# Two reordered places and POOL's divisions in a two-layer attention and expert kernel

## What is computed

```
block 0: linear attention, 32 heads of 64
block 1: mixture of experts
block 2: softmax attention, 32 query heads of 8, 8 key/value heads
    scores = einsum(q, k) / sqrt(8);  attn = softmax(scores)
    out = einsum(attn, v);            return out @ Wo + bo
block 3: mixture of experts
    expert = argmax(x @ router);  xs = x * sigmoid(max logit)
    out = (silu(xs @ gate[e]) * (xs @ up[e])) @ down[e]      for each token's expert e
    shared = (silu(x @ sgate) * (x @ sup)) @ sdown;          return out + shared
```

## Time and profile before

| | us |
|---|---|
| median of 3 runs | 669.4 |
| lowest, highest of them | 667.64, 670.4 |
| profiled execution, device time | 665.62 |
| its span (first to last instruction) | 663.9 |
| PE, DVE, ACT, POOL busy in the span | 615.3, 400.0, 328.4, 208.7 |
| TensorE's granted clock, mean of the span | 0.983 |

### The profile page before, as it was taken

The page is one execution under the profiler, slowest core; times in us unless marked ns, Lnnn a source line. Parts: engine busy times, 40 slices in busy tenths (PEclk is TensorE's granted clock), DMA queues, the critical chain, the costliest instruction groups (busy, mean ns, idle before and its releaser), DMA issues.

```text
span 663.9 us, 11796 instructions
## 1 busy us (share of the span) xinstructions
PE 615.3 (93%) x4298; PEld 407.6 (61%) x4298; DVE 400.0 (60%) x929; ACT 328.4 (49%) x654; POOL 208.7 (31%) x304
## 2 busy tenths in 40 slices
PE   3999999999999988999879999999999999999980
PEld 2887887888888785566566444444444445556650
DVE  5426705632760577443377989888899955743335
ACT  4523423433332234254315588898988875423321
POOL 5870661282074064313422122111010100431331
PEclk9999999999999999999979999999999999999995
DMA  6100200300199996314199996000000000031213
GB/s 221 33 1 33 96 1 25 102 1 1 34 272 271 119 176 223 105 48 120 69 296 335 270 155 4 1 2 1 2 1 2 1 2 1 17 106 47 84 53 126
DMA packets 69000, 57.40 MB, mean 86 GB/s; under 512 B 21520, under 2 KB 64400, under 8 KB 68944
## 3 DMA queue, kind: packets, MB, share of 16 engines
q1 hardware_dynamic: 66736, 50.60, 34.0%
q0 software_dynamic: 2208, 6.05, 2.5%
HBM read 30.78 MB, written 25.85 MB: 85 GB/s over the span
## 4 chain that ended last, share of the span: by engine, by line
PE 76%; DVE 15%; ACT 3%; DMA 2%; issue 2%; POOL 2%; ACTq 0%; POOLq 0%; SPq 0%; DVEq 0%
PE psum L303 9%; PE psum L305 9%; PE psum L304 9%; PE psum L1296 8%; PE psum L1641 8%; DVE mx L1751 7%; PE psum L1325 5%; PE psum L1613 5%; PE psum L1601 5%; PE psum L1626 3%; PE psum L1289 3%; DVE stat L652 2%; PE psum L1220 2%; PE psum L1571 2%; PE psum L1305 1%
## 5 line engine op out<-in xcount | busy, mean ns | idle before, releaser
L1751 DVE TENSOR_REDUCE mx<-psum 128x1 f32<-128x512 f32 x256 | 157.7, 683 | 17.5 <-PE psum L1613 17.4
L1512 ACT ACTIVATE pr<-psum 128x512 f32<-128x512 f32 x256 | 137.8, 599 | 28.2 <-PE psum L1626 26.4
L1641 PE MATMUL psum<-pr,vals 128*32 128x256 f32 x1024 | 77.6, 389 | 0.0
L1626 PE MATMUL psum<-qT,kT 32*128 32x512 f32 x256 | 76.5, 494 | 0.7 <-ACT pr L1512 0.7
L1613 PE MATMUL psum<-kT,qT 32*128 32x512 f32 x256 | 67.7, 489 | 1.7 <-ACT qT L1479 0.7
L1296 PE MATMUL psum<-w_gu,xgT 128*128 x120 | 56.4, 592 | 0.0
L610 POOL DMA_INDIRECT routed_y<-yr,xg x30 | 28.8, 958 | 87.8 <-DVE yr L862 87.2
L1613 PEld LDWEIGHTS psum<-kT,qT 32*128 32x128 f32 x256 | 26.3, 182 | 43.9 <-issue 21.0
L1553 POOL CAST mp<-mx 128x16 bf16<-128x16 f32 x16 | 3.1, 196 | 150.6 <-DVE mx L1751 150.6
L853 DVE SCALAR_TENSOR_TENSOR h<-psum,xg,sg 128x256 f32<-128x256 f32 x30 | 14.5, 484 | 49.8 <-ACT sg L1051 49.8
L999 ACT ACTIVATE q<-psum 128x512 f32<-128x512 f32 x32 | 19.1, 596 | 48.9 <-PE psum L305 48.9
(11 more groups left out here) (214 smaller groups left out, 1391.7 us busy)
## 6 DMA issues: line engine op xcount, KB each, us to landing
sorted_x<-zeros SPq DMA_DIRECT2D x2, 9088.0 KB, 45.3
w_gu<-in_L_ffn_gate_w SPq DMA_DIRECT2D x16, 256.0 KB, 6.3
w_gu<-in_L_ffn_up_w SPq DMA_DIRECT2D x16, 256.0 KB, 6.4
w_d<-in_L_ffn_down_w SPq DMA_DIRECT2D x16, 256.0 KB, 6.2
xg<-sorted_x SPq DMA_DIRECT2D x30, 129.0 KB, 2.2
wk_f<-in_L_attn_Wk SPq DMA_DIRECT2D x4, 512.0 KB, 5.2
wq_f<-in_L_attn_Wq SPq DMA_DIRECT2D x4, 512.0 KB, 5.9
wv_f<-in_L_attn_Wv SPq DMA_DIRECT2D x4, 512.0 KB, 3.9
```

What stands on the lines that cost most here:

```text
L1512: nc.scalar.activation(pr[d % 3][:, j], s2_bank(d, j), ACT.Exp, scale=SCALE).then_inc(exp_ready, 1)
L1626: mm(s2_bank(d, j), kT[n // GH][rows, kc * P:(kc + 1) * P], qT2[n % 2][rows, :], start=True, stop=True).then_inc(s2_made, 1)
L1641: last = mm(ps[AV_BANK][j * VW:(j + 1) * VW, cols], vals[:, n // NKV * TB + kc, n % NKV // GH * GH + j, :], pr[d % 3][:, j, cols], start=( ...
L1751: v.tensor_reduce(mx[n % 2][:, t, j:j + 1], s1_bank(c, j), AX.X, ALU.max, negate=True).then_inc(max_read, 1)
```

## The change

It does three things.

1. At loop turn 22 of the experts (`NU - 1`) `down(20)` and `down(21)` move ahead of `gate_up(22)` on PE, and `take_down(20)` and `take_down(21)` move ahead of `gated(22)` on DVE. This holds for both layers.
2. In the attention loop "q1" is turned in step 4n in place of 4n + 2, with the same group number, ahead of "o". Step 4n + 2 has no turn any more. ACT copies it in the same step.
3. For groups 0 to 12 DVE only copies the nine columns from PSUM to a new buffer `taken` (two of them), and POOL divides: a power with exponent -1 of the 16 sums, then a product. POOL does this for group n - 3 after it has handed over the maxima of group n. Groups 13 to 15 are divided by DVE as before. A new semaphore `att_taken` counts DVE's reads, and `att_ready` now counts POOL's results.

```diff
 dve_moe:    for i in range(3, NU + 1):
+                if i == NU - 1:
+                    for u in downs_at(i):
+                        take_down(u)
                 if i < NU:
                     gated(i)
-                for u in downs_at(i):
-                    take_down(u)
+                if i != NU - 1:
+                    for u in downs_at(i):
+                        take_down(u)
 pe_moe:         if i == NU - 1:
                     turn_h(i - 1)
+                    for u in downs_at(i):
+                        down(u)
                 if i < NU:
                     gate_up(i)
...
-                for u in downs_at(i):
-                    down(u)
+                if i != NU - 1:
+                    for u in downs_at(i):
+                        down(u)
 turns_at(c):
             if c % TB == 0:
-                what = ("o", (c - 12) // TB)
+                what = [("q1", c // TB + 1), ("o", (c - 12) // TB)]
             elif c % TB == 1:
-                what = ("q2", (c - 5) // TB)
-            elif c % TB == 2:
-                what = ("q1", c // TB + 1)
+                what = [("q2", (c - 5) // TB)]
+            elif c % TB == 3:
+                what = [("k", (c + 5) // 16 if (c + 5) % 16 == 0 else NG)]
 pool_l1_loop:
+            def divide(n):
+                pool.wait_ge(att_taken, n + 1)
+                pool.wait_ge(att_chain, n + 1)
+                g.tensor_tensor(over[:], taken[n % 2][:, :, :, HD:HD + 1], minus[:], ALU.pow).then_inc(att_chain, 1)
+                pool.wait_ge(att_chain, n + 2)
+                g.tensor_tensor(att_of(n), taken[n % 2][:, :, :, 0:HD], over[:].to_broadcast([P, TB, GH, HD]),
+                                ALU.mult).then_inc(att_ready, 1)
             for n in range(NG):
...
+                if n >= 3:
+                    divide(n - 3)
 turn_att(t):
                 if t < TB:
-                    pe.wait_ge(att_ready, LATE_O)
+                    pe.wait_ge(att_taken, LATE_O)
+                    pe.wait_ge(att_ready, NKV)
...
                 else:
-                    pe.wait_ge(att_ready, NG)
+                    pe.wait_ge(att_taken, NG)
+                    pe.wait_ge(att_ready, LATE_O)
 outputs(n):
-                link(v.reciprocal(dn[:], o[:, :, :, HD]))
-                v.tensor_tensor(
+                if n < LATE_O:
+                    if n >= 2:
+                        dve.wait_ge(att_ready, n - 1)
+                    v.tensor_copy(taken[n % 2][:], o[:, :, :, 0:HD + 1]).then_inc(att_taken, 1)
+                else:
+                    link(v.reciprocal(dn[:], o[:, :, :, HD]))
+                    v.tensor_tensor(att_of(n), o[:, :, :, 0:HD], dn[:].unsqueeze(3).to_broadcast([P, TB, GH, HD]),
+                                    ALU.mult).then_inc(att_taken, 1)
```

More of the change, by code:

```diff
@@ L220, in build @@
         dn = at("dn", [P, TB, GH], F32, l1)
+        taken = [at(f"taken{i}", [P, TB, GH, HD + 1], F32, l1) for i in range(2)]
+        over, minus = (at(n, [P, TB, GH, 1], F32, l1) for n in ("over", "minus"))
         qT1 = [at(f"qT1_{i}", [P, S], F32R, l1_in_y) for i in range(2)]
@@ L291, in build @@
         av_done, oT_ready, att_ready = sem("av_done"), sem("oT_ready"), sem("att_ready")
+        att_taken, att_chain = sem("att_taken"), sem("att_chain")
         attT_made, proj_made = sem("attT_made"), sem("proj_made")
@@ L1378, in turns_at @@
             if c % TB == 0:
-                what = ("o", (c - 12) // TB)
+                what = [("q1", c // TB + 1), ("o", (c - 12) // TB)]
             elif c % TB == 1:
-                what = ("q2", (c - 5) // TB)
-            elif c % TB == 2:
-                what = ("q1", c // TB + 1)
-            else:
-                what = ("k", (c + 5) // 16 if (c + 5) % 16 == 0 else NG)
-            return [what] if 0 <= what[1] < (NKT if what[0] == "k" else NG) else []
+                what = [("q2", (c - 5) // TB)]
+            elif c % TB == 3:
+                what = [("k", (c + 5) // 16 if (c + 5) % 16 == 0 else NG)]
+            else:
+                what = []
+            return [x_ for x_ in what if 0 <= x_[1] < (NKT if x_[0] == "k" else NG)]
         END = STEPS + LAG + 3
@@ L1417, in bank_no, with att_of @@
             return AV_BANK if item == FIRST[0] else TURN_BANK
+        def att_of(n):
+            b, half, h_ = n // NKV, n % NKV // GH, n % GH
+            return xn[:, b * TB:(b + 1) * TB, :].rearrange("p t (s r h d) -> p t s r h d", s=2, r=GH,
+                                                           d=HD)[:, :, half, :, h_, :]
         def s1_bank(c, j):
@@ L1443, in wait_read @@
             if what[0] == "o":
-                eng.wait_ge(att_ready, BY_READER["dve"].index(what) + 1)
+                eng.wait_ge(att_taken, BY_READER["dve"].index(what) + 1)
             else:
@@ L1541, in second_batch @@
                 stack_lo(g, 1, t, "q").then_inc(q_stacked[1], 1)
+            g.memset(minus[:], -1.0).then_inc(att_chain, 1)
+            def divide(n):
[5 more added lines that the diff above has]
+                                ALU.mult).then_inc(att_ready, 1)
             for n in range(NG):
@@ L1753, in outputs @@
             def outputs(n):
-                b, half, h_ = n // NKV, n % NKV // GH, n % GH
                 dve.wait_ge(turned, turn_no(("o", n)))
                 o = ps[bank_no(("o", n))].rearrange("p (t h w) -> p t h w", t=TB, h=GH)
-                link(v.reciprocal(dn[:], o[:, :, :, HD]))
-                v.tensor_tensor(
-                    xn[:, b * TB:(b + 1) * TB, :].rearrange("p t (s r h d) -> p t s r h d", s=2, r=GH, d=HD)[:, :, half, :, h_, :],
-                    o[:, :, :, 0:HD], dn[:].unsqueeze(3).to_broadcast([P, TB, GH, HD]), ALU.mult).then_inc(att_ready, 1)
+                if n < LATE_O:
[6 more added lines that the diff above has]
+                                    ALU.mult).then_inc(att_taken, 1)
             def l1_y(t):
```

## The result

The changed kernel takes 660.8 us (median of four runs, 659.8 to 660.9) against 668.8 us for the kernel before in the same comparison (667.6 to 670.4). The ratio is 0.9856, with a 95% interval of 0.9826 to 0.9886. It is 1.4% faster, which is clear of the noise, and the forecast of 661.5 us (658.0 to 665.5) holds. The 7.9 us of the forecast, taken from this comparison's own 668.8, would give 660.9. The profiled execution took 660.8 us, with a span of 659.0.

What follows compares the result with a forecast made beforehand. The prediction took PE and DVE waiting for each other to bound the loop, and a late last store the experts' end. 3.4 (experts' end) + 4.5 (loop) + 0 (division) = 7.9 us off the 669.4 median gives 661.5 us, range 658.0 to 665.5.

Steps and rivals of the forecast that it cites:

- The bound: Attention loop: a group's 11.30 us closes over PE and DVE waiting for each other, with DVE's division outside that sum.
- The experts' end: End of the experts, both layers: last store's data 1.71 us sooner with `down` ahead of `gate_up(22)`, 3.4 us in all.
- The turn: Attention loop, "q1" moved to step 4n: period 10.88 us, 0.40 gained per group; 4.5 us for the loop, bounds 3.0 and 5.5.
- The term of the "k" groups: Two loop groups with a "k" turn in step 4n + 3: about 11.5 us against 11.74, 2 x 0.25 = 0.5 us gained.
- The division: Attention loop, division moved to POOL: DVE saves 0.27 us per group, 3.5 us in all, booked at nothing; cost 0.
- the estimate that stood beside the sum: POOL's product in the division: some 0.6 us by the skill page's half of VectorE's speed, not used in the sum.
- that cover stays: After "o" in the loop: DVE's next maximum still waits for PE's first scores, hiding DVE's outputs; otherwise 3.5 us would count.
- (e): Attention loop: POOL's division stops DVE's maxima while it lasts, 13 x up to 4.8 = 62 us, about 723 us; chance 0.02.
- (a): Attention loop: "q1" holds "o" back by what it frees in step 38; only the experts' 3.4 remain, 666.0 us; chance 0.14.
- (b): Attention loop: DVE's outputs lie on the path once PE is ahead, 3.5 us more gained, 658.0 us; chance 0.06.
- (c): Experts' end: half the gain, because the stores' pace or the landing takes over, 663.2 us; chance 0.07.
- (d): Step 40: ACT's added copy delays step 41's second scores, 12 x 1.08 = 13 us lost, 3.4 gained, 679 us; chance 0.05.

Runs made afterwards that it cites:

- the reciprocals: Experts' end and "q1" turn moved, DVE dividing with three or seven reciprocals for one, against the kernel before: 661.16 us (ratio 0.9895) and 672.66 us (1.0086).

## Why the prediction was right, and where it was off

**The bound.** The prediction closed the group's loop over PE and DVE, with two of PE's waits in it, and took DVE's division out of that loop. Both hold: before, "o" starts 0.05 us behind DVE's maximum in every group, with the turn alone the period falls from 11.31 to 10.90, and with the division alone it doesn't move.

**The experts' end: right.** It said that the last store would start 1.71 us sooner; it starts 1.69 us sooner in each layer. The predicted steps from one store to the next, 1.26 and 1.26, are 1.33 and 1.26. The data gave 1.70 in the first layer and 1.48 in the second, since there the first sum comes 5.83 us behind the last store's start instead of 5.62. In the other profiles that distance is 5.31 to 5.71 us, moved unit or not, so the missing 0.2 is most likely the spread of the landing. So 3.2 came in the place of 3.4. Unit 22 was to end its take 1 us ahead of the sum; it ends 1.8 us ahead, since it moved back by 1.2 us behind the transposes and not by 1.7.

**The turn: right in its sum, with PE's own need put too low.** A group without a "k" turn, and not behind one, was to last 10.88 to 10.90 and lasts 10.89 to 10.91. The unbroken run from step 4n + 1's second half, the missing pause and the longer one behind the outputs (near 0.6 predicted, 0.64 measured) all show. But the prediction let DVE set the new period, at 10.88, and gave PE a need of 10.77. PE needs 10.9. In the kernel after, its step 32 goes from 444.94 to 448.44, 3.50 where 3.40 was booked: 0.42 and not 0.35 from the second pair of first scores to "o", and 0.47 and not 0.43 ahead of the turn, where ACT's ring takes a few hundredths. Steps 34 and 35 take 2.30 each. That 10.90 lies so near to DVE's 10.88 is luck; the bounds of 0.30 to 0.42 for each group allow a period of up to 11.0.

The term of the "k" groups, 0.25 us each, seems mis-sized when one counts from first maximum to first maximum: they gain 0.54 (11.74 to 11.20), and the groups behind them, and group 3 behind the turn of step 11, gain 0.15 (11.15 to 11.16 now) where 0.40 were booked. That is the marker and not PE. DVE's first maximum shows only half of the delay in the "k" group and the rest in the next. From "q1" turn to "q1" turn a "k" group takes 11.44, a gain of 0.30, and the group behind it 10.92, a gain of 0.40. A "k" turn has 0.59 us of work; it cost 0.44 before, when PE had waits to take it up, and costs 0.54 now. The twelve groups gained 4.35 by their first maxima for the 4.5 predicted. Groups 0 and 2 were to lose 0.3 and give it back; they lost 0.12 and gave 0.08, with 0.05 lost in group 1.

**The division: right.** POOL's power takes 2.90 us, within the 1.03 to 4.1 that stood as bounds and nearer to their upper end; it takes neither a fixed time nor four times that of the small one. The product takes 0.41 (at most 0.73 predicted, and some 0.6 by the estimate that stood beside the sum), DVE's copy 0.29 (0.30), and the division ends 6 us ahead of the next group's maxima on POOL. It costs nothing and gives nothing. The step "that cover stays" was measured by the reciprocals: 0.8 us with DVE's own division.

**The two engines side by side.** Rival (e) had a division stop the maxima. The maxima at 448.98 take 1.29 for two while the power of 447.36 to 450.26 is under way, just as at 461.88 in the earlier trace rows without one, and the run of 14 at 450.57 keeps its 0.60 us start to start beside the product. Of the 30 maxima that lie wholly inside a power the longest takes 0.692 us, and the longest of the kernel before 0.693. The rule of the Trainium skill that was cited for it ("SBUF — State Buffer", section "SBUF: two separate sides") agrees with these rows, now for a POOL instruction longer than four maxima.

**The rivals.** (a) The stall only moves: its price fell, with the twelve groups at 132.2 us. Its premise was nearer to the truth than the forecast's: PE has nothing left in the new period, and "o" waits for PE's own sequence. It lost because PE needs 10.9 and not 11.3. ACT's three banks, which spoke for it, end the pause of 0.28 ahead of the turn, of which 0.25 would stand there without them. (b) DVE's outputs on the path: fell by the division alone. (c) Half of the experts' gain: fell with 1.69. (d) ACT becomes the bound: it keeps 0.22 us of pause at 447.54 where it had 0.59 in the earlier trace rows and the prediction left it 0.10, so it missed by a little more than foreseen. (e) fell as told. The time ahead of the changed places differed from one execution to the next by as much as a rival's effect, and only places inside the kernel could be compared to 0.1 us.

## What to carry to other kernels

Close the loop that repeats, engine by engine and wait by wait, before you price an edit: a turn of 0.59 us that moved was worth 0.40, the distance to the next bound, and 3.4 us of work taken off an engine outside that loop were worth nothing and came back as 3.4 us of waiting. When the edit leaves an engine with nothing to spare, irregular work on it is paid nearly in full: 0.54 of a "k" turn's 0.59 us, where it was 0.44. A pause that the profile puts down to another engine need not be a wait: see whether the same pause stands where nothing is waited for, and how long before it the awaited work had ended. To learn how much room is left, put known work on the engine in two doses, one under the expected cover and one over it.

## What was not expected of the hardware

- TensorE's granted clock fell to half in the middle of the loop, in some executions of a program and not in others, behind stretches of 3 or 4 us in which it was still 2.44 of 3 or 3.44 of 4 us busy. Group 2 lasted 13.34 us instead of 10.57, and the kernel's last part 132.1 instead of 126.5. A stretch with a granted clock of 0.50 is TensorE at 1.2 GHz. The Trainium skill ("TensorE: Matmul & The Clock Gate", section "Part 1: The HAM clock gate") says that the gate grants either half or full rate; the stretches agree, since all values between stand at the edges of a fall. It also ties the gate to how busy TensorE has been of late. The rows ahead of the falls fit that, but the same load passed without a fall in five other profiles of the moved turn, and 2.34 of 3 us in two of the old order.
- A power on POOL takes 1.03 us for 128x4 elements and 2.90 for 128x16, so 1.87 us for the twelve further columns, 0.156 each; an estimate from these two sizes leaves about 0.4 that is fixed. A product of 128x128 with a broadcast factor takes 0.41, a seventh of the power before it.
- Seven dependent reciprocals of 128x16 on DVE take 2.00 us, 0.28 to 0.29 each.
